# First phase of a two-layer gated cross-attention kernel: context's rounding step, x1's squares and the order of VectorE's work

## What is computed

```python
x = x + tanh(g_xattn[0]) * xattn0(layernorm(x), ctx)  # both rounded to fp8, x by 1x128 blocks, ctx by 128x128 blocks
x = x + tanh(g_ffn[0]) * ffn0(layernorm(x), w0, gamma)  # rms norm, 8-bit rows by one global maximum, ternary weights
x = x + tanh(g_xattn[1]) * xattn1(layernorm(x), ctx, ctx)  # softmax(q k) v in 8 heads
x = x + tanh(g_ffn[1]) * ffn1(layernorm(x), router_w, Wa, Wb)  # top 2 of 8 experts of rank 128
```

## Time and profile before

| what | value |
|---|---|
| median of 3 runs | 2164.76 us |
| profiled execution: time / span of the core | 2161.88 us / 2159.8 us |
| mean granted TensorE clock | 0.962 of full |
| busy over the span | PE 87%, DVE 74%, ACT 59%, POOL 39% |
| first phase: 0 to 567.3 us; second phase | 1592.5 us |
| busy between 100 and 400 us, per 100 us | DVE 97, PE 80 to 84, ACT 71 to 77, POOL 58 to 60 |

### The profile page before, as it was taken

The page is one execution under the profiler, slowest core; times in us unless marked ns, Lnnn a source line. Parts: engine busy times, 40 slices in busy tenths (PEclk is TensorE's granted clock), DMA queues, the critical chain, the costliest instruction groups (busy, mean ns, idle before and its releaser), DMA issues.

```text
span 2159.8 us, 26457 instructions
## 1 busy us (share of the span) xinstructions
PE 1881.5 (87%) x8968; PEld 846.1 (39%) x8968; DVE 1601.8 (74%) x2369; ACT 1273.0 (59%) x2059; POOL 836.2 (39%) x1154
## 2 busy tenths in 40 slices
PE   0586979877568999999999999999999999999997
PEld 0232434433223444444444444444444444444443
DVE  6899999987456777777777777777777777777761
ACT  3676768765255565565656556565555656565650
POOL 2465555564123433333333333334333333333320
PEclk9998989998768999999999999999999999999998
DMA  7465656587457888878887877888877787878781
GB/s 176 136 178 155 194 147 173 132 223 181 130 113 141 172 158 169 152 153 169 161 171 156 169 154 154 170 158 172 154 159 166 153 164 160 174 156 169 132 154 41
DMA packets 923462, 339.96 MB, mean 157 GB/s; under 512 B 849472, under 2 KB 898624, under 8 KB 923328
## 3 DMA queue, kind: packets, MB, share of 16 engines
q1 hardware_dynamic: 917504, 335.40, 72.4%
q10 hardware_dynamic: 5824, 2.88, 0.6%
HBM read 92.83 MB, written 33.55 MB: 59 GB/s over the span
## 4 chain that ended last, share of the span: by engine, by line
DVE 35%; issue 20%; ACT 18%; PE 12%; POOL 9%; DMA 4%; SPq 0%; POOLq 0%; ACTq 0%; DVEq 0%
ACT slot L784 8%; DVE tiny L1329 7%; DVE tiny L1051 5%; POOL tiny L631 5%; ACT arena L776 4%; POOL tiny L629 3%; ACT tiny L770 2%; DVE slot L1333 2%; DMA slot<-slot 2%; PE sc L889 2%; DVE slot L1065 2%; DVE arena L1341 2%; DVE slot L1316 2%; PE sc L947 2%; DMA probs<-slot 2%
## 5 line engine op out<-in xcount | busy, mean ns | idle before, releaser
L1333 DVE SCALAR_TENSOR_TENSOR slot<-arena,tiny,slot 128x1024 f16<-128x1024 f32 x256 | 328.3, 1283 | 316.6 <-ACT slot L784 316.6
L947 PE MATMUL sc<-arena,slot 128*128 128x512 f16 x1536 | 378.1, 387 | 33.3 <-ACT arena L776 23.6
L784 ACT ACTIVATE slot<-arena,tiny 128x1024 f16<-128x1024 f32 x256 | 293.7, 1147 | 180.3 <-POOL tiny L631 166.8
L629 POOL TENSOR_SCALAR tiny<-tiny 128x1 f32<-128x1 f32 x256 | 99.4, 388 | 699.2 <-ACT arena L776 699.2
L1329 DVE TENSOR_REDUCE tiny<-sc 128x1 f32<-128x1024 f32 x256 | 306.1, 1205 | 15.3 <-PE sc L947 13.8
L776 ACT ACTIVATE arena<-sc,tiny,head_tab 128x1024 f32<-128x1024 f32 x256 | 308.4, 1205 | 8.6
L770 ACT ACTIVATE tiny<-tiny,head_tab 128x1 f32<-128x1 f32 x256 | 73.9, 289 | 351.2 <-DVE tiny L1329 351.2
L947 PEld LDWEIGHTS sc<-arena,slot 128*128 128x128 f16 x1536 | 151.5, 99 | 223.6 <-ACT arena L776 29.1
L889 PE MATMUL sc<-probs,slot 128*128 128x512 f16 x768 | 179.2, 396 | 47.7 <-DMA slot<-slot 44.1
L963 PE MATMUL accs<-probs,arena 128*128 128x512 f16 x512 | 194.5, 380 | 12.7 <-issue 12.6
L930 PE MATMUL accs<-wb_hi,slot 128*128 128x512 f16 x512 | 195.1, 381 | 8.6 <-DMA slot<-slot 8.6
(11 more groups left out here) (211 smaller groups left out, 3137.2 us busy)
## 6 DMA issues: line engine op xcount, KB each, us to landing
arena<-in_x SPq DMA_DIRECT2D x32, 512.0 KB, 3.7
x_scratch<-arena SPq DMA_DIRECT2D x32, 512.0 KB, 3.0
slot<-x_scratch SPq DMA_DIRECT2D x32, 512.0 KB, 3.9
slot<-in_ctx SPq DMA_DIRECT2D x32, 512.0 KB, 4.2
out<-arena SPq DMA_DIRECT2D x32, 512.0 KB, 3.4
slot<-in_L_ffn_weight SPq DMA_DIRECT2D x12, 512.0 KB, 4.1
slot<-in_L_ffn_Wa SPq DMA_DIRECT2D x12, 512.0 KB, 4.6
slot<-in_L_ffn_Wb SPq DMA_DIRECT2D x12, 512.0 KB, 4.8
```

The costliest lines, as they stand in the source:

```text
L784: act.activation(PH[c % 2], PF[c % 2], ACT.Identity, scale=rinv[c % 2][:]).then_inc(s_ph.sem, 1)
L947: mm = pe.matmul(sc[:, c % 2, h * HALF:(h + 1) * HALF], q[i][:, c * P:(c + 1) * P], k[j][:, h * HALF:(h + 1) * HALF], start=start, stop=stop)
L1333: dve.scalar_tensor_tensor(out=PL[c % 2], in0=PF[c % 2], scalar=rinv[c % 2][:], in1=PH[c % 2], op0=ALU.mult, op1=ALU.subtract).then_inc(s_ ...
```

## The change

Context: ACT no longer scales a tile in place (`c_scale`); it writes `|c * factor * 2^20|` as bfloat16 into a step buffer (`c_abs`). DVE takes the maximum of that with a constant (`c_step`) and then does scaling and addition in one operation (`c_add`); the mask operation on context is gone. Both step buffers are doubled. The tile of `SQ` in SBUF becomes the twelfth slot of the context ring; ACT writes x1's squares into two PSUM banks, where DVE multiplies them. The fill of a context tile now has only the other two banks and comes in halves: four matmuls, one eviction of both parts, four matmuls, one eviction, with half a product of 24 matmuls between the halves. On DVE all operations that read two SBUF tensors, and the rounding operations, stand in one block at the start of a step; weight preparation on DVE comes one step later and stands behind that block. `xsafe` and `xk` become operations with one tensor input on columns two floats apart. POOL's list becomes x_round, c_round, x_rstd, x_low. ACT's list is reordered. The first column loads (now 12 tiles) are all issued by SP. The context runs one step less ahead.

```diff
...
-FIRST, LAST = -11, TILES + 1
-C_SCALE, C_ROUND, C_FILL, C_EVICT, C_MAX = 11, 10, 9, 8, 19
+FIRST, LAST = -10, TILES + 1
+C_ABS, C_ROUND, C_FILL, C_MAX = 10, 9, 8, 19
-X_RING, C_RING = 7, 11
+X_RING, C_RING = 7, 12
 GROUPS, GROUP_ROWS, CHUNK = 16, 64, 8
-TABLE_STEPS = tuple(PER_BATCH * b - 11 for b in range(1, B))
...
+HALF_CHUNK = CHUNK // 2
+TABLE_STEPS = tuple(PER_BATCH * b - C_ABS for b in range(1, B))
+C_GROUPS = ((0, 4), (4, 4), (8, 3), (11, 1))
+C_PAIRS = {12: 2, 13: 0, 14: 2, 15: 0}
 STAT_STEPS = 21
...
-        XSTEP, CSTEP = XS.bitcast(BF16)[:, 0:D], slot[3][:].bitcast(BF16)[:, 0:D]
+        XSTEP, CSTEP = [[t.bitcast(BF16)[:, i * D:(i + 1) * D] for i in range(2)] for t in (XS, slot[3][:])]
         XC = [slot[i] for i in range(3)]
-        SQ, GSQ = slot[4], slot[10]
+        GSQ = slot[10]
...
-        C = [ring[:, i] for ring in rings for i in range(4)][:C_RING]
+        C = [ring[:, i] for ring in rings for i in range(4)][:C_RING - 1] + [slot[4][:]]
...
+        apart = [small(2 * KB).rearrange("p (k two) -> p k two", two=2)[:, :, 0] for i in range(6)]
+        xam, xrec, xsafe, xk = apart[0], apart[1], apart[2:4], apart[4:6]
+        xt2 = small(KB)
...
-        fills = accs[:].rearrange("p a n -> p (a n)")
-        filled = fills.rearrange("p (r t k s) -> p t k s r", r=CHUNK, t=2, k=KB)
+        fills, SQ = (accs[:, i:i + 2, :].rearrange("p a n -> p (a n)") for i in (0, 2))
+        filled = fills.rearrange("p (r t n) -> p t n r", r=HALF_CHUNK, t=2)
+        w_out = [w.rearrange("p t k (s r) -> p t (k s) r", s=GROUPS) for w in w_both]
+        w_turn, w_spread = accs[0:4, 0, 0:P], accs[:, 1, 0:4]
...
+            return [t for t in range(3 * KB) if j == (t - KB if t < KB else (t - KB) * STAT_STEPS // (2 * KB))]
...
+                for k in range(KB):
...
             for j in range(FIRST, LAST + 1):
...
                 if is_x(j + 2) and j + 2 >= X_EARLY:
                     x_round(j + 2)
                 if is_c(j + C_ROUND):
                     c_round(j + C_ROUND)
+                if is_x(j + 4) and j + 4 >= X_EARLY:
+                    x_rstd(j + 4)
+                if is_x(j + 2) and j + 2 >= X_EARLY:
+                    x_low(j + 2)
+                if j == -4:
+                    pool.wait_ge(gates.sem, 1)
+                    c_tables(0)
...
-            for g, (first, count) in enumerate(C_GROUPS):
-                for k in range(KB // 2, KB):
-                    load_c_columns(act, first, count, k, c0_in[g])
...
-            def c_scale(m):
+            def c_abs(m):
                 b, i = divmod(m, PER_BATCH)
                 if i == 0:
                     act.wait_ge(cf_k.sem, cf_k.at(b))
-                act.activation(C[m % C_RING], C[m % C_RING], ACT.Identity, scale=crk[:, b % 2:b % 2 + 1])\
-                   .then_inc(c_v.sem, 1)
-
-            def c_evict(m):
+                after(act, c_q, m - 2)
+                act.activation(CSTEP[m % 2], C[m % C_RING], ACT.Abs, scale=cstep[:, b % 2:b % 2 + 1]).then_inc(c_a.sem, 1)
+
+            def c_evict(m, half):
                 b, i = divmod(m, PER_BATCH)
-                act.wait_ge(c_fill.sem, c_fill.at(m))
+                act.wait_ge(c_fill.sem, c_fill.at(m, half + 1))
                 if i == 0:
                     after(act, mm1, (b - 1) * PER_BATCH - 1)
+                r = i * CHUNK + half * HALF_CHUNK
+                act.activation(w_out[b % 2][:, :, :, r:r + HALF_CHUNK], filled, ACT.Identity, scale=1.0 / FILL)\
+                   .then_inc(c_out.sem, 1)
...
+                if j == -5:
+                    act.wait_ge(const_in.sem, 48)
+                    act.activation(gate[:], gate_in[:], ACT.Tanh).then_inc(gates.sem, 1)
+                    act.activation(GSQ[:], gamma_b[:], ACT.Square).then_inc(gsq.sem, 1)
...
                 if is_x(j + 1) and j + 1 >= X_EARLY:
                     x_high(j + 1)
-                if is_c(j + C_EVICT):
-                    c_evict(j + C_EVICT)
+                if is_c(j + C_FILL):
+                    c_evict(j + C_FILL, 0)
+                if is_c(j + C_ABS):
+                    c_abs(j + C_ABS)
+                for t in stats_of(j):
+                    weight_stat(t)
                 if is_x(j + 3) and j + 3 >= X_EARLY:
                     x_scale(j + 3)
+                if is_c(j + C_FILL):
+                    c_evict(j + C_FILL, 1)
+                if is_x(j - 1):
+                    x1_square(j - 1)
                 if is_x(j + 4) and j + 4 >= X_EARLY:
                     centre(j + 4)
-                if is_c(j + C_SCALE):
-                    c_scale(j + C_SCALE)
-                if is_x(j - 1):
-                    x1_square(j - 1)
-                for t in stats_of(j):
-                    weight_stat(t)
...
-            def fill(m):
+            def fill(m, half):
                 b, i = divmod(m, PER_BATCH)
...
+                if half == 0:
+                    pe.wait_ge(c_q.sem, c_q.at(m))
+                    after(pe, c_out, m - 1)
...
+                else:
+                    pe.wait_ge(c_out.sem, c_out.at(m, 1))
+                for i in range(HALF_CHUNK):
+                    r = half * HALF_CHUNK + i
+                    mm = pe.matmul(fills[:, 2 * i * P:2 * (i + 1) * P], CQ[m % 2][:, r * P:(r + 1) * P], diag[:, b % 2, :],
                                    start=True, stop=True)
                 mm.then_inc(c_fill.sem, 1)
...
+                if is_c(j + C_FILL):
+                    fill(j + C_FILL, 0)
                 if is_x(j):
                     if j % PER_BATCH == 0:
-                        pe.wait_ge(c_lo.sem, c_lo.at(j + PER_BATCH - 1))
+                        pe.wait_ge(c_out.sem, c_out.at(j + PER_BATCH - 1))
                     pe.wait_ge(x_turned[j % 2].sem, x_turned[j % 2].at(j // 2))
                     after(pe, e_x1, j - 2)
                     product(j, range(KB // 2))
-                if j in TABLE_STEPS:
-                    c_spread_max((j + 11) // PER_BATCH)
+                if is_c(j + C_FILL):
+                    fill(j + C_FILL, 1)
+                if is_x(j):
+                    product(j, range(KB // 2, KB)).then_inc(mm1.sem, 1)
+                if j + 1 in TABLE_STEPS:
+                    c_spread_max((j + 1 + C_ABS) // PER_BATCH)
...
+            def c_step(m):
+                s = CSTEP[m % 2]
+                dve.wait_ge(c_a.sem, c_a.at(m))
+                dve.tensor_scalar(s, s, FP8_MIN_NORMAL * ROUND_FP8, None, ALU.max).then_inc(c_s.sem, 1)
+
+            def c_add(m):
+                b, i = divmod(m, PER_BATCH)
+                if i == 0:
+                    dve.wait_ge(cf_k.sem, cf_k.at(b))
+                dve.wait_ge(c_s.sem, c_s.at(m))
+                dve.scalar_tensor_tensor(out=C[m % C_RING], in0=C[m % C_RING], scalar=crk[:, b % 2:b % 2 + 1],
+                                         in1=CSTEP[m % 2], op0=ALU.mult, op1=ALU.add).then_inc(c_u.sem, 1)
...
+                dve.tensor_scalar(xsafe[i], xam, xrstd[:, i:i + 1], ACT_EPS, ALU.mult, ALU.max).then_inc(x_am.sem, 1)
...
+                dve.tensor_scalar(xk[i], xrec, xrstd[:, i:i + 1], FP8_MAX, ALU.mult, ALU.mult).then_inc(x_k.sem, 1)
 
...
+                dve.tensor_scalar(cstep[:, i:i + 1], crec[:], FP8_MAX * STEP_FP8, None, ALU.mult).then_inc(cf_k.sem, 1)
...
+                next_x = is_x(j + 2) and j + 2 >= X_EARLY
+                if j in TABLE_STEPS:
+                    c_factors((j + C_ABS) // PER_BATCH)
+                if j == PREP - 2:
+                    weight_widest()
+                if j == PREP - 1:
+                    weight_factors()
+                if j == PREP:
+                    router_split()
+                if next_x:
+                    x_factors(j + 2)
+                if is_c(j + C_ROUND):
+                    c_step(j + C_ROUND)
+                if next_x:
+                    x_mask(j + 2)
+                if is_c(j + C_ROUND):
+                    c_add(j + C_ROUND)
+                if next_x:
+                    x_step(j + 2)
+                    x_add(j + 2)
+                if PREP < j <= PREP + KB:
+                    ternary_round(j - PREP - 1)
+                    weight_low(j - PREP - 1)
                 if is_x(j + 3) and j + 3 >= X_EARLY:
                     x_max(j + 3)
                 if is_x(j + 4) and j + 4 >= X_EARLY:
                     x_stats(j + 4)
                 if is_x(j - 2):
+                    if j == 2:
+                        dve.wait_ge(gsq.sem, 1)
                     x1_max(j - 2)
-                if j == PREP - 1:
-                    weight_factors()
-                if is_x(j + 2) and j + 2 >= X_EARLY:
-                    x_round_start(j + 2)
-                if j in TABLE_STEPS:
-                    c_factors((j + 11) // PER_BATCH)
-                if is_c(j + C_ROUND):
-                    c_round_start(j + C_ROUND)
                 if is_x(j - 1):
                     finish_x1(j - 1)
                 for m in maxima_of(j):
                     c_max(m)
```

(9 more changed lines are left out.)

167 lines of the change are left out of this document (66 added, 101 removed).

## The result

The changed kernel takes **2142.74 us** (median of 4 runs, 2140.23 to 2143.24), against 2164.47 for the kernel before beside it: a ratio of 0.9898, 95% interval 0.9881 to 0.9915. It is 21.7 us faster. The prediction was 2099 us, a gain of 65.8. The direction was right, and a third of the gain came.

A forecast was written before the change was run, and what follows sets the result against it. The prediction took VectorE's list, with its waits for GpSimd over SBUF, to bound the first phase. Its terms, 17.5 + 50.3 + 7.5 - 9.5 = 65.8 us gained, gave a median of 2099 us, range 2083 to 2150.

The forecast's parts named there:

- What bounds the kernel: First phase: VectorE's list sets the time, and its order and GpSimd's decide how often they exclude each other from SBUF.
- A full step: VectorE's step falls from 14.07 to 11.9 us, set by GpSimd's loop; bounds 11.5 and 14.4.
- rival (a): Full steps: xsafe and xk wait beside GpSimd's roundings; 14.4 us with c_max, 13.6 without, about 2144 us in all; chance 0.20.
- Points 1 and 2: Before step 0: start section gains 10 us, context-only steps 7.5, so step 0 begins at 81.4 us instead of 98.9.
- Point 1: Start section: ScalarE issues no transfers, so centring can begin at about 6 us, not 16.85; gain 10, bounds 5 and 12.
- The fill chain: Context-only steps: fill, evict, fill, evict takes 4.15 us a step, in place of 4.66 us steps.
- Point 3: Steps 0 to 21: 270 us in place of 320.3, with two sets of factors at 9; gain 50.3.
- Rival (b): Steps 2 to 11: SyncE sets the pace, 14.1 and 13.65 us instead of 11.9; 2114 us in all; chance 0.10.
- (c): Full steps: evictions of the halves come too late, TensorE stands 6.6 us, step 18.0; 2235 us in all; chance 0.05.
- (d): Full steps: VectorE's block does not stay whole and the step stays 14.07 us; about 2149 us in all; chance 0.05.
- Point 4: Steps 22 to 27, with weight preparation at 14.6 us a step: 79.5 us in place of 87.0; gain 7.5, bounds 0 and 14.
- Point 5: Step 28 to barrier: SyncE's ternary transpose waits about 8 us for VectorE; 70.5 us against 61; loss 9.5, bounds 3 and 15.

The follow-up runs named there:

- e15: The changed kernel with one bfloat16 mask over 1024 columns put back ahead of context's step on VectorE: 2157.8 us.
- e5: The changed kernel with the small operations (xsafe, its reciprocal, xk) moved from right behind x_max to behind x1_max: 2127.0 us.
- e4: The changed kernel with the 24 weight statistics spread over steps 0 to 20 again, instead of eight of them in steps -8 to -1: 2128.9 us.
- e12: The changed kernel with the first column loads again issued half by SyncE and half by ScalarE: 2151.2 us.
- e7: e5 with the weight statistics spread as in e4: 2121.9 us.
- e13: The changed kernel with SyncE issuing the transpose of a ternary block one step later: 2140.8 us.
- e14: e7 with small operations behind x_stats from step 24, no statistics in steps 6 to 11, batch-maximum transpose before a product's last quarter, ternary transpose one step later: 2105.3 us.
- e16: e14 with SyncE's three weight loads issued behind the next load and transposes of x, not ahead of them: 2099.6 us.
- e1: The changed kernel with xsafe, its reciprocal and xk moved from right behind x_max to behind finish_x1, the end of VectorE's list: 2154.8 us.
- e6: No kernel: a bare list of 15 small VectorE forms, each timed with GpSimd idle and beside a GpSimd subtraction of two SBUF tensors; no total time given.
- e3: The changed kernel with xsafe, the reciprocal and xk made over nine columns side by side, the ninth an unused constant: 2145.9 us.

## Why the prediction was wrong

**What bounds the kernel: right.** VectorE's list and its waits for GpSimd. A mask counts in full (e15), and the wait of context's step went.

**A full step: the term that failed.** "7.0 follow that do not contend" counted xsafe and xk without a wait. They wait 0.85 and 1.58 us, and they stand where GpSimd's two roundings always run. The prediction had this as rival (a), priced at 14.4 and 13.6 us a step; measured 13.61 and 12.70. It gave it 0.20, with the one-column L1174, which never waits, as the evidence against, though no row had eight columns. The row that was nearer was L1065 in the same group, one source, SBUF to SBUF, which does wait. Rival (a) was dearer than what happened, 45 us against 28.5: its waits were 2.9 a step and not 2.4, and VectorE's sum without them 11.5 and not 13.61 - 2.4 = 11.2. That its total met the measured time within 2 us is chance, since the start lost 19.4 besides.

The rest of the step's mechanism stands. With the waits mostly gone (e5), GpSimd's loop sets the step without c_max, as forecast, at 11.28 us and not 11.9: its block is 4.24 and not 4.6, its work 7.03 and not 7.3. With c_max VectorE's own list sets it, at 11.56. The stretch is 28.5 us of the 46 by which the profiled barrier missed the forecast. e5 has 277.2 us for it, so 21.3 of the 28.5 go with the two waits. In what remains two errors work against each other: shorter steps than forecast, and c_factors, forecast at 9 us for two sets and costing 8.2 in the changed kernel but some 21 once the steps are short.

**Points 1 and 2: 19.4 us short, by two causes.** The larger is a misreading of the prediction's own diff. It said that the steps with two loads for statistics are seven of steps 0 to 7; the diff puts one statistic into each of steps -8 to -1. There they put ScalarE behind the landing of the weights and c_abs behind ScalarE: 13.5 us (e4), a wait to which the prediction gave no term. Point 1's mechanism holds: ScalarE's first operation comes at 6.2 us, in place of 16.85, and e12 shows that this counts. But the first c_factors gain 6.0 us (L1157 at 38.3, the same line, L1143, at 44.3 before) and not 10. From loads of 0.76 us each and 290 GB/s the first four tiles were to be there at 13 us; the 0.76 is the price of SyncE's first four loads in the kernel before (3.06 us; the next four took 8.71). Now SyncE took 9.15 us to issue the first eight, 1.14 each, and VectorE waited for them until 17.5 (whether the issue or the transfer was late is not shown):

```profile
1.64 9.15 SPq L316 DMA_DIRECT2D tern<-in_ctx  x8
```

```profile
17.54 4.60 DVE L1131 TENSOR_REDUCE slot<-tern 128x1 f32<-128x1024 f32 x4 [4.75 <-DMA tern<-in_ctx]
```

The second rounding of x waits for GpSimd here as it did in the kernel before (3.6 us in all, against 3.8), so it is no part of the miss. The fill chain was sized well: 4.37 us a step (e4) against 4.15. With e4's list step 0 starts at 87.3, and the two small items (4 and 9 x 0.22) explain the difference to 81.4.

**Point 3's other terms.** c_add, in place of an addition of 1.22, takes 1.28; x1_max through PSUM 1.21, against 1.17: 0.04 more where the bounds were 0 to 0.1. Rival (b) did not show, since VectorE was slow enough, and came up as soon as it was fast (e7). Rivals (c) and (d) did not happen. TensorE did stand for evictions in full steps, mostly 0.25 to 1.9 us, but not the 6.6 a step of rival (c), and these waits are gone in the ordinary steps of e5, which suggests that they followed from the slow step; the step of context (L1086) has a median of 0.42 us.

**Point 4: right**, in size and in mechanism: 78.5 against 79.5, and 14.86 us for each of steps 25 to 27 against 14.6. ternary_round's second operation (L1234) waits for x_round, 2.50 us at the median against 0.69 alone.

**Point 5: right in size, wrong in cause.** 69.6 against 70.5. The transpose of the ternary block is worth 2 us (e13), not 8. Read from x_max of step 28 the end did not grow at all, 58.9 us against 61.0: in the table it is longer because the changed kernel's step opens 10.7 us ahead of x_max there. Why the end is not shorter still was not taken apart. The load of x behind three weight loads (e14 to e16) costs time in steps 25 to 27 of the faster versions and none in the end; in the changed kernel x_stats does not wait for it.

One thing stays untried: x1's squares back in SBUF. The ring's twelfth slot has taken their room.

## What to carry to other kernels

An operation of VectorE that takes 0.2 us can wait as long as one of 1024 columns: when two engines exclude each other, count waits by the kind of each operation and by what the other engine does at that moment, not by size. Moving such an operation has two limits, the end of the other engine's work and the engine that waits for the result; e1 and e5 differ by 28 us for one position in a list. And when the bound of a step is removed, list what stood just below it: here GpSimd's loop at 11.3 us a step with TensorE at 11.2 under it, SyncE's queue at 13 and the order of two loads came up one after another. Write the order of a list down from the diff, step by step: 13.5 us were lost by eight operations that the prediction had placed eight steps too late.

## What the runs showed of the hardware

Beside a GpSimd operation that reads two SBUF tensors, a tensor_scalar from SBUF to SBUF waits with 7, 8 and 9 columns (7 and 8: 1.5 us in e6 for 0.15 to 0.22 alone; 9: 1.8 us in e3 for 0.23), at both distances between columns tried, and not with one; a reciprocal of eight columns (0.19 us) and a tensor_scalar of eight that has its source or its result in PSUM (0.21) do not. The Trainium skill (SBUF — State Buffer, "Who interferes with whom") names copies, casts and tensor_scalar, under conditions on their operands, and the operations with two SBUF inputs as those that contend, and reductions as those that never do; all forms tried agree (copies and casts were not), and the reciprocal, which that list leaves out, behaves as a reduction does.

A load of 512 KB issued 0.7 us behind three others of that size was there 7.3 us after its issue, in e14. VectorE waited for such a load 2.35 and 2.05 us in steps 26 and 27, and in neither when it was issued first.
